# TensorE's ring of PSUM banks: eight banks up to the second attention's first step, six from there on

## What is computed

```python
x = x + 0.5 * _L0_ffn_ref(_layernorm(x), ...)   # 8 experts, top 2, plus a shared expert, SwiGLU
x = x + _L0_attn_ref(_layernorm(x), ...)        # 32 heads, linear attention, group norm
x = x + 0.5 * _L0_ffn_ref(_layernorm(x), ...)
x = x + 0.5 * _L1_ffn_ref(_layernorm(x), ...)   # 8 experts of width 32, top 1, GELU
x = x + _L1_attn_ref(_layernorm(x), ...)        # 8 heads, gated recurrence M = M*f + g*k v^T, y = q M * o
x = x + 0.5 * _L1_ffn_ref(_layernorm(x), ...)
```

## Time and profile before

| | us |
|---|---|
| three runs | 1602.87, 1611.95, 1610.63 (median 1610.63) |
| the profiled execution, its span | 1611.3 |
| of it TensorE busy with matmuls | 1208.2 (75%) |
| VectorE / ScalarE / GpSimd busy | 1037.9 / 881.7 / 645.2 |

### The profile page before, as it was taken

How to read it: one execution, slowest core, us unless ns; L and a number is a source line. 1 busy time by engine, 2 the same in 40 slices (tenths; PEclk the granted TensorE clock), 3 DMA queues, 4 the chain that set the end, 5 groups by cost and what they waited for, 6 DMA issues and landing times.

```text
span 1611.3 us, 37336 instructions
## 1 busy us (share of the span) xinstructions
PE 1208.2 (75%) x14084; PEld 950.7 (59%) x14113; DVE 1037.9 (64%) x3441; ACT 881.7 (55%) x1505; POOL 645.2 (40%) x679
## 2 busy tenths in 40 slices
PE   3745767567766778767666766799989897989997
PEld 2423545455555666555554645677877676768776
DVE  7954655455645656666664664677767757888774
ACT  3545556334544445645543653676677445766764
POOL 1364443344555455555545453431322323342100
PEclk9876878787887978988887887898898978999989
DMA  8012323223132322222132222311210101010001
GB/s 263 14 50 62 79 68 75 59 63 83 57 84 70 78 71 76 62 65 55 57 87 67 68 67 66 76 43 46 56 46 23 28 18 33 15 29 24 2 9 34
DMA packets 172875, 93.77 MB, mean 58 GB/s; under 512 B 98516, under 2 KB 163183, under 8 KB 172575
## 3 DMA queue, kind: packets, MB, share of 16 engines
q1 hardware_dynamic: 115886, 35.64, 9.0%
q0 software_dynamic: 16384, 33.59, 7.3%
q10 hardware_dynamic: 40432, 22.17, 4.9%
HBM read 25.78 MB, written 45.61 MB: 44 GB/s over the span
## 4 chain that ended last, share of the span: by engine, by line
PE 37%; DVE 22%; ACT 13%; another core or an unknown queue 13%; issue 12%; POOL 1%; DMA 1%; ACTq 0%; POOLq 0%; DVEq 0%; SPq 0%
PE bank L759 8%; PE bank L581 3%; PE bank L820 2%; PE bank L967 2%; PE bank L806 2%; PE bank L839 2%; DVE x L1135 2%; PE bank L775 2%; PE sums L984 1%; PE sums L901 1%; PE bank L532 1%; PE sums L904 1%; ACT heads_store L1674 1%; DVE heads_store L1189 1%
## 5 line engine op out<-in xcount | busy, mean ns | idle before, releaser
L1914 POOL DMA_INDIRECT rows<-store,r_slot x256 | 258.8, 1011 | 185.1 <-DVE r_slot L1396 114.1
L759 PE MATMUL bank<-u_xp,w_hi 128*128 128x128 f16 x2432 | 267.3, 237 | 83.7 <-issue 74.0
L1930 POOL DMA_INDIRECT y_in<-ys,r_result x256 | 262.2, 1024 | 120.6 <-issue 70.3
L759 PE MATMUL bank<-u_xp,w_lo 128*128 128x128 f16 x1216 | 245.7, 237 | 34.6 <-issue 34.4
L759 PEld LDWEIGHTS bank<-u_xp,w_hi 128*128 x2432 | 212.3, 108 | 100.0 <-issue 94.4
L759 PEld LDWEIGHTS bank<-u_xp,w_lo 128*128 x1216 | 130.3, 107 | 47.1 <-issue 47.1
L581 PE MATMUL bank<-heads_store,w_hi 128*128 128x512 f16 x256 | 92.6, 449 | 7.0 <-DVE r_lg L1164 4.2
L1874 POOL TENSOR_SCALAR ve_last<-mv_last 128x4 f32<-128x4 f32 x16 | 3.1, 195 | 215.0 <-DVE mv_last L1092 214.9
L1698 ACT ACTIVATE heads_store<-bank,sc 128x512 f32<-128x512 f32 x64 | 43.3, 682 | 75.0 <-PE bank L581 41.1
L1135 DVE SCALAR_TENSOR_TENSOR x<-y_in,r_weight,x 128x128 f32<-128x128 f32 x256 | 72.5, 346 | 1.1
L1189 DVE TENSOR_TENSOR heads_store<-bank,heads_store 128x512 f32<-128x512 f32 x64 | 43.7, 686 | 42.7 <-ACT heads_store L1698 33.9
(11 more groups left out here) (434 smaller groups left out, 3478.4 us busy)
## 6 DMA issues: line engine op xcount, KB each, us to landing
ys<-u_y_even ACTq DMA_DIRECT2D x38, 256.0 KB
ys<-u_y_odd ACTq DMA_DIRECT2D x38, 256.0 KB
u_xp<-rows SPq DMA_TRANSPOSE x304
x<-x_dram SPq DMA_DIRECT2D x16, 256.0 KB, 5.6
rows<-store,r_slot POOLq DMA_INDIRECT x256
y_in<-ys,r_result POOLq DMA_INDIRECT x256
out_dram<-x SPq DMA_DIRECT2D x16, 256.0 KB
rows<-blank SPq DMA_DIRECT2D x48, 64.0 KB
```

The costliest lines, as they stand in the source:

```text
L759: ins = pe.matmul(B[:, of_block[j]], of_expert(wp, e, F16, part, which), xp_rows[:, xp, of_block[j]], start=(n == 0 and j == 0), stop=(n = ...
L1914: pool.indirect_dma_start(row_dram[g], bass.IndirectOffsetOnAxis(route.slot[g][:, i, t:t + 1].bitcast(U32), 0), rows[:, groups[g].first * ...
L1930: pool.indirect_dma_start(fetch.y[i][:, t, k, :], None, y_dram[g], bass.IndirectOffsetOnAxis(route.result[g][:, k, t0 + t:t0 + t + 1].bitc ...
```

## The change

The ring gets all eight banks, the two `sums` as its last two. At the first step of the second attention's front (`c == 0 and k == 0`) it is cut to the six (`narrow`), going on at the next of them in turn, and the signals that free the last contents of the other two are kept in `lent`. The back's first step 2, the first that writes to `sums`, waits for these. `warm` no longer asks whether the attention has begun.

```diff
--- before.py
+++ after.py
@@ -93,10 +93,11 @@
 
 
     def __init__(self, banks):
-        self.banks, self.n, self.freed, self.of = banks, 0, [None] * len(banks), {}
+        self.all, self.of = banks, {}
+        self.restart()
 
     def restart(self):
-        self.n, self.freed = 0, [None] * len(self.banks)
+        self.banks, self.n, self.freed = self.all, 0, [None] * len(self.all)
 
     def take(self, *use):
         k = self.n % len(self.banks)
@@ -108,11 +109,18 @@
         k = self.n % len(self.banks)
         return self.banks[k], self.freed[k]
 
+    def narrow(self, n):
+        k = self.n % len(self.banks)
+        while k >= n:
+            k = (k + 1) % len(self.banks)
+        self.banks, self.n = self.all[:n], k
+        return self.freed[n:]
+
     def free_at(self, use, signal, *point):
         self.freed[self.of[use]] = (signal, point)
 
     def __getitem__(self, use):
-        return self.banks[self.of.get(use, 0)]
+        return self.all[self.of.get(use, 0)]
 
 
 class Group:
@@ -249,7 +257,7 @@
 
         banks = [ctx.enter_context(nc.psum_tensor(f"bank{k}", [P, N], F32)) for k in range(6)]
         sums = [ctx.enter_context(nc.psum_tensor(f"sums{u}", [P, T, P], F32)) for u in range(2)]
-        ring = Ring(banks)
+        ring = Ring(banks + [u[:].rearrange("p t n -> p (t n)") for u in sums])
 
         def lane(name):
             s = Lane(name)
@@ -517,7 +525,7 @@
         def tensor_program(pe):
             on = Waiting(pe)
             ring.restart()
-            held, carried = {}, []
+            held, lent = {}, []
 
             def bank(*use):
                 b, freed = ring.take(*use)
@@ -824,6 +832,8 @@
 
             def attn1_front(c, k):
                 s = front
+                if c == 0 and k == 0:
+                    lent.extend(ring.narrow(len(banks)))
                 if k == 0:
                     on.wait_ge(*mids[c % 2].by_vector.at("ffn1", c))
                     M = bank(s.name, "xn", "attn1", c)
@@ -890,9 +900,11 @@
                 if k in (0, 1):
                     scores(c, k)
                 elif k == 2:
-                    carried.append(c)
                     if c:
                         on.wait_ge(*s.by_scalar.at("yot", c - 1))
+                    else:
+                        for signal, point in lent:
+                            on.wait_ge(*signal.at(*point))
                     on.wait_ge(*front.by_vector.at("sth", c))
                     on.wait_ge(*front.by_scalar.at("qdt", c))
                     for u in range(2):
@@ -988,13 +1000,10 @@
                 s.by_tensor.mark(ins, "values", c, quad)
 
             def warm():
-                if carried:
-                    into, freed = ring.next()
-                    if freed:
-                        on.wait_ge(*freed[0].at(*freed[1]))
-                    into = into[:, 0:T * HALF].rearrange("p (t n) -> p t n", t=T)
-                else:
-                    into = sums[0][:, :, HALF:D]
+                into, freed = ring.next()
+                if freed:
+                    on.wait_ge(*freed[0].at(*freed[1]))
+                into = into[:, 0:T * HALF].rearrange("p (t n) -> p t n", t=T)
                 pe.matmul(into, ident_b[:], ident_b[:, 0:HALF].unsqueeze(1).broadcast_to([P, T, HALF]),
                           start=True, stop=True, skip_group_check=True)
 
```

## The result

The changed kernel takes 1601.28 us, the median of 10 runs (1586.89 to 1605.26), beside 1611.29 us for the kernel before (10 runs, 1602.87 to 1615.58). The ratio is 0.9924, with a 95% interval of 0.9899 to 0.9949: faster by 0.76%, some 12 us, and by the medians 10.0 us. The forecast was 1604.6 us: the measured time lies inside its range of 1590 to 1615 us, and the sign is right, but 6 us of gain were forecast where 10 to 12 came. Single runs of one kernel lie 13 to 37 us apart, so every reading of one profiled execution needs a second one.

The account below looks back on a forecast made before the run. Bound by results handed between TensorE and its readers, with an unnamed delay; two thirds of 8.9 us, 6 us, off 1611.3 gives 1605.3 us profiled, 1604.6 us as median; range 1590 to 1615 us (8 in 10).

Parts of the forecast that it names:

- The waits that go: At seven takes in the first 998 us, waits for the reader six back vanish; idle times there total 15.1 us.
- What a wait is worth: At bank takes before 998 us, a wait gives at most its idle time; takes off the chain give nothing by themselves.
- The place: Of 8.9 us counted at seven takes, 1.89 and 0.24 us lie at 220.09 and 394.32 us, the rest later.
- The discount for late results: At 220.09, 394.32 and 902.72 us only time since the last late result counts, so 15.1 us becomes 8.9 us.
- Rival A: In the first 998 us all 15.1 us returns, nearby takes off the chain being cleared too: 1595.5 us; chance 25%.
- B: Late results take up what the banks give; TensorE then waits for split rows or statistics: 1610.6 us; chance 27%.
- C: First 998 us: bunched idle time brings more 1.2 GHz stretches, 3.1 us each; 1623 us with four, no gain; chance 10%.
- The waits for lines 1164 and 1698 gone: TensorE's waits for these readers at lines 581 and 759 should be gone or nearly so in the first stretch.
- "Remote" as before: ScalarE's idle time ended by "remote" should stay about as it was; shrinking by over 10 us would favour Rival A.
- Sums 6 us earlier: The attention's first matmul to `sums` should start some 6 us earlier than 1051.5 us.
- The stretch behind them as before: From the attention's first `sums` to the end, the time should last as before.
- The added wait before the sums: The first write to `sums`, at 1051 us, waits for the two banks' last readers, long done: costs 0.

Follow-up runs that it names:

- the four kernels six deep throughout: The kernel before; its ring of six begun at bank 2 (0.9946) or bank 4 (1.001); eight banks, each take waiting for the reader six back (1.0008).
- the rotation by four: The kernel before with its ring of six begun at bank 4 instead of bank 0, no wait moved: 1588.89 us, 1.001 of the kernel before.
- the first half: Eight banks up to take 336 of 714 (near 500 us), six from there on: 1576.78 us, 0.9914 of the kernel before.
- the one deep at the two places: Eight banks, waiting for the reader six back except at 15 takes (about 319 to 324 and 447 to 455 us), eight back there: 1.0031 of the kernel before.
- the four deep profiles: The changed kernel (0.9924), it measured again (0.990), seven banks (0.9912), and eight banks kept until the sums are written (0.9939), all against the kernel before.
- the second measurement: The changed kernel run again beside the kernel before, with the experiments: 1569.58 us beside 1588.21 us, 0.990 (6 runs).

## Why the prediction was right, and where not

**The waits that go.** Right. At all seven places of the sum TensorE's idle time is gone in both profiles of the changed kernel. At 737.30 us it is 1.70 to 1.71 us in all six profiles that are six deep there and none in the six that are deeper; at 902.72 us it is 1.8 to 2.5 us and none. The readings of single rows were less firm: at 394.32 us the four kernels six deep throughout have 4.16, 2.87, none and 2.70 us.

**What a wait is worth.** This is the step that failed: "Takes off the chain give nothing by themselves", and a wait on the chain gives at most its own length. At 322 us a wait of 0.47 us, too small for the sum, gave 4.1 us. At 902 us a wait of 2.5 us gave 2.5, just its length. And at 737 us, the step from 730 to 757 us became longer. Here is what became of the 1.7 us there, in two kernels on one chip. First the rotation by four, then the changed kernel: TensorE, then VectorE or the matmul that waits for it, with lines 1310 and 1319 the same reading of a result.

```profile
736.31 0.40 PE L772 MATMUL bank<-by_expert,r_member 128*128 128x128 bf16 x4 [1.70 <-ACT u_gated_odd L1769]
...
748.60 0.42 DVE L1310 TENSOR_TENSOR kvm_head<-bank,w_packed 128x256 f32<-128x256 f32 x1 [1.20 <-remote]
...
749.08 1.13 PE L619 MATMUL bank<-heads_store,kvm_head 128*128 128x256 f32 x4 [2.32 <-DVE kvm_head L1310]
```

```profile
710.92 0.39 PE L780 MATMUL bank<-by_expert,r_member 128*128 128x128 bf16 x4
...
727.74 0.42 DVE L1319 TENSOR_TENSOR kvm_head<-bank,w_packed 128x256 f32<-128x256 f32 x1 [4.35 <-remote]
...
728.22 2.07 PE L627 MATMUL sums<-heads_store,kvm_head 128*128 128x256 f32 x4 [5.09 <-DVE kvm_head L1319]
```

The wait of 1.70 us is gone, and a result behind it is read after 4.35 us of idle time instead of 1.20. The later result isn't the price of the missing wait, though: the two other kernels that are six deep here and deep before (the first half, and the one deep at the two places) keep the wait and take 28.3 us for this step as well. What the rows do show is that results are late by a few us more or less whatever this wait does, so that its 1.7 us can't be read as a gain. A bank wait that goes shifts the work behind it by a us or less, and at 322 us that decided whether results came late by 7 us. What a small shift is worth can't be read off the wait.

**The place.** Wrong. 6.8 of the 8.9 us counted lay after 500 us. Eight banks in the first half alone measured the whole gain, 0.9914, where the sum had 2.1 us. Eight in the second half alone measured 1.0027 [0.9988, 1.0066], with the slip told above. That the whole came out inside the range is so far luck: most of the gain came where the sum had little.

**The discount for late results.** The row was read rightly: around 394 us, where it took 4.16 us down to 0.24, the four six-deep and the four deep profiles take 14.8 us each on average from 386.7 to 402 us (difference 0.0, standard error 0.4). But lateness was used only to make terms smaller. It can also make them larger, as at 322 us.

**The size.** 6 us forecast, 10 to 12 measured (16 in the second measurement), above the 8.9 us that stood as the upper bound, though both intervals (8 to 16 us and 7 to 25) reach down to it. Rival A's 15.1 us is at least as near as the forecast, but its reasons aren't borne out: in the profiled pair ScalarE's "remote" idle time stayed (268 and 269 us), where A wanted it to shrink by over 10, and the clock hardly moved (0.82 and 0.83). Over the four and four profiles of the table that idle time is 268 and 257 us, with a standard error of 6, so one pair was too little for this sign, and A's mark is neither met nor missed. B fell with the interval. C fell: the clock is not below 0.80.

**The signs named ahead.** The waits for lines 1164 and 1698 gone: yes. "Remote" as before: yes in the pair, open over the eight profiles. Sums 6 us earlier: 3.3 us in the profiled pair, 8 us on average between four and four profiles with a standard error of 9, which can't be told from either. The stretch behind them as before: 6.5 us shorter in the pair, 3.4 with a standard error of 2.4 over the eight, though nothing differs there. The added wait before the sums: it isn't among the waits, 0 as forecast.

## What to carry to other kernels

More PSUM banks in a ring can pay even where the waits for banks are 1% of the span, and one more may be enough; but here the wait's length said neither how much nor where. Give the ring its old waits with the new banks to tell depth from placement, and lay the start times of the same instructions of several profiles side by side: a difference that all of one kind show at one place is worth more than a sum of rows from one profile. Take in the profiles made for another purpose too: the third difference above looks like one of the depth until two of them stand beside it. Where a reader's idle time ends with "remote" and TensorE's matmul had long been done, look at GpSimd's indirect DMAs first: here plain DMAs in place of half of them gave over ten times what the banks gave, in a kernel that no longer gathers.

## What the hardware did that I had not expected

A reader of TensorE's results stood idle for up to 20 us (ScalarE, `u_gated_odd`, the kernel before) while GpSimd issued indirect DMAs of about 1 us each in a dense row, and 33 of the 50 long waits of this kind ended within 2.6 us after such a row. Replacing 256 of the 512 indirect DMAs halves that idle time (268 to 137 us). TensorE's own matmuls come one by one in such a row, with 0.3 to 0.5 us of idle time between them in the lines shown, and nothing that the profile shows them waiting for. The lateness isn't random: it struck the same result, by 5.8 to 6.5 us of TensorE's idle time ahead of line 591, in all six kernels six deep at that place and in none of the other six, in profiles from four sets of runs.
